# Second layer of a three-layer kernel: output with the tokens on the partitions, states spread in groups of four tiles, and the additions of the lag products on GpSimd

## What is computed

```
ctx      = causal_ema(x, tau_ctx)
gated    = x * sigmoid([x, ctx] @ Wg.T + bg)
h1       = gelu(x @ Wn1.T + bn1)
mod      = 0.5 + sigmoid(h1 @ Wn2.T + bn2)                 # one value per token and trace
traces_d = causal_ema(gated * mod_d, tau_d)                # 32 traces, a = exp(-softplus(tau_d))
temporal = sum_d blend_w[d] * traces_d
gate     = sigmoid(temporal @ Wtemp.T + btemp)
soma     = gelu(x @ Wsoma.T + bsoma)
out      = (soma * gate) @ Wout.T
x        = x + (out - mean(out)) / sqrt(var(out) + 1e-5) * gamma + beta
```

## Time and profile before

| | |
|---|---|
| runs | 2219.94, 2221.18, 2221.75 us; median 2221.18 |
| the profiled execution | span 2220.5 us from the first to the last instruction; its time outside the profiler is not given apart from the three above |
| layer 1, layer 2, layer 3 | about 0 to 938, 938 to 1704, 1704 to 2220 us |
| busy over the span | PE 2051.3 (92%), DVE 1699.0 (77%), ACT 1196.2 (54%), POOL 796.4 (36%) |
| mean granted clock of PE | 0.974 of full speed |

### The profile page before, as it was taken

How to read it: one execution, slowest core, us unless ns; L and a number is a source line. 1 busy time by engine, 2 the same in 40 slices (tenths; PEclk the granted TensorE clock), 3 DMA queues, 4 the chain that set the end, 5 groups by cost and what they waited for, 6 DMA issues and landing times. The chain is left out here.

```text
span 2220.5 us, 42789 instructions
## 1 busy us (share of the span) xinstructions
PE 2051.3 (92%) x14158; PEld 1652.1 (74%) x14158; DVE 1699.0 (77%) x2530; ACT 1196.2 (54%) x2428; POOL 796.4 (36%) x589
## 2 busy tenths in 40 slices
PE   3899999999999999759999999999995999999998
PEld 2566666666666666447777777777774999999997
DVE  6788888888888888577878888887875566666664
ACT  2466565666665666435555555555554555555553
POOL 4645444444455554033333333333340111111111
PEclk8999999999999999879999999999997999999998
DMA  3444444444444444100000000000001222222221
GB/s 92 106 106 107 107 110 110 108 109 108 105 105 106 108 109 104 24 25 1 0 0 0 0 0 0 0 0 0 0 0 59 78 79 70 85 69 80 85 66 60
DMA packets 121171, 137.47 MB, mean 62 GB/s; under 512 B 24240, under 2 KB 89776, under 8 KB 121136
## 3 DMA queue, kind: packets, MB, share of 16 engines
q1 hardware_dynamic: 118576, 128.64, 22.9%
q0 software_dynamic: 2560, 8.39, 1.0%
HBM read 48.35 MB, written 8.39 MB: 26 GB/s over the span
## 5 line engine op out<-in xcount | busy, mean ns | idle before, releaser
L366 DVE TENSOR_REDUCE a_neg_max<-a_s 128x2 f32<-128x512 f32 x512 | 329.1, 683 | 123.4 <-PE a_s L613 121.8
L487 ACT ACTIVATE a_e<-a_t 128x512 f32<-128x512 f32 x512 | 281.2, 610 | 228.4 <-PE a_t L626 228.4
L375 DVE SCALAR_TENSOR_TENSOR a_e<-a_e,a_w_t 128x1024 f32<-128x1024 f32 x256 | 373.6, 1469 | 4.1 <-ACT a_e L487 4.1
L613 PE MATMUL a_s<-a_k_st,a_q_st 96*128 96x256 f32 x1024 | 275.4, 380 | 0.0
L613 PEld LDWEIGHTS a_s<-a_k_st,a_q_st 96*128 96x128 f32 x1024 | 203.5, 199 | 13.7
L610 PE MATMUL a_s<-a_add_m,ident_bf 128*128 128x512 bf16 x512 | 201.8, 394 | 7.9 <-POOL a_add_m L254 5.8
L1695 ACT ACTIVATE c_hid<-c_pH,c_b 128x256 f32<-128x256 f32 x256 | 107.4, 471 | 186.3 <-PE c_pH L1758 185.9
L897 POOL TENSOR_TENSOR b_decayed<-b_table,b_mod_t 128x1024 f32<-128x1024 f32 x64 | 118.6, 1872 | 210.3 <-ACT b_mod_t L1163 203.0
L1317 PE MATMUL b_pS<-b_gated_t,b_decayed 128*128 128x256 f32 x768 | 189.5, 390 | 0.7
L626 PE MATMUL a_t<-a_q_st,a_k_st 97*128 97x512 f32 x512 | 177.1, 426 | 2.6 <-DMA a_q_st<-a_max_row 2.0
L642 PE MATMUL a_v<-a_e,a_v_pad 128*32 128x256 f32 x2048 | 163.6, 392 | 4.5 <-DVE a_e L375 2.1
(11 more groups left out here) (261 smaller groups left out, 5720.4 us busy)
## 6 DMA issues: line engine op xcount, KB each, us to landing
a_q_st<-a_q_hi SPq DMA_DIRECT2D x256, 128.0 KB, 2.4
a_k_st<-a_k_hi SPq DMA_DIRECT2D x256, 64.0 KB, 2.0
a_q_st<-a_q_lo SPq DMA_DIRECT2D x128, 128.0 KB, 2.4
a_xs<-in_xT SPq DMA_DIRECT2D x32, 256.0 KB, 2.8
a_k_st<-a_k_lo SPq DMA_DIRECT2D x128, 64.0 KB, 2.1
x_all<-in_xT SPq DMA_DIRECT2D x32, 256.0 KB, 2.8
c_we<-in_we SPq DMA_DIRECT2D x32, 256.0 KB, 2.7
c_key_t<-in_keyT SPq DMA_DIRECT2D x32, 256.0 KB, 3.2
```

The source lines that it names most:

```text
L366: dve.tensor_reduce(neg_max[:, qc, head:head + 2], ps_s[b][:], AX.X, ALU.max, negate=True).then_inc(red_done, 1)
L375: dve.scalar_tensor_tensor(out=buf[:], in0=buf[:], scalar=BIG, in1=w_t[par][:, kc].unsqueeze(1).to_broadcast([P, 4, S]), op0=ALU.min, op1= ...
L487: act.activation(e[g % E_BUFS][:, 2 * b:2 * b + 2], ps_t[b][:], ACT.Exp).then_inc(exp_done, 1)
L613: ins = pe.matmul(ps_s[b][:, r], q_st[par][0:96, slot, qc * P:qc * P + P], k_st[par][0:96, slot // 2], start=False, stop=(r == 1))
```

## The change

In the trace layer alone:
- `output` swaps its operands: the mixed activations are stationary and `Wout` moves, so `b_pZ` has the tokens on the partitions. The sum of squares over the channels is then along the free axis: ACT's Square with `accum_out` gives `var`, 128x2, and the matmuls of `mean_square` go. The root and the reciprocal are of 128x2. `normalized` (two ACT copies with a scale per partition, into `normed`, which lies in the tile of `wtemp`) takes the place of DVE's product, and `turn_normed` (four PE transposes, into `b_pB`) brings the channels back to the partitions. `scaling` reads `b_pB` and writes `scaled`, which lies in the tile of `wsoma`.
- `spread` is called twice with four tiles instead of four times with two, with four `state` buffers.
- The additions of the lag products are POOL's (`lag_add`), between its low parts and `residual`, with `decays` in the middle.
- The orders of PE, DVE, ACT and POOL are written anew.

```diff
@@ POOL
+        def lag_add(n, lag):
+            pool.wait_ge(prod_done, STEP * n + lag + 1)
+            if lag > 1:
+                pool.wait_ge(inner_done, (STEP - 1) * n + lag - 1)
+            pr = rows(prod[lag % 2]).rearrange("p (a j) -> p a j", j=STEP)[:, :, 0:STEP - lag]
+            y = rows(inner).rearrange("p (a j) -> p a j", j=STEP)[:, :, lag:STEP]
+            pool.tensor_tensor(y, y, pr, ALU.add).then_inc(inner_done, 1)
         def body(n, par, has_a, has_c):
             if has_a:
-                low_inputs(n + 1, 1 - par)
+                low_x(n + 1, 1 - par)
+                low_context(n + 1)
+            for lag in range(1, 5):
+                lag_add(n, lag)
+            if has_a:
                 decays(n + 1, 1 - par)
+            for lag in range(5, STEP):
+                lag_add(n, lag)
             if has_c:
                 residual(n - 1)
@@ DVE
+            if lag > 2:
+                dve.wait_ge(inner_done, (STEP - 1) * n + lag - 2)
             dve.tensor_tensor(pr, g[:, :, 0:STEP - lag], m[:, :, 0:STEP - lag], ALU.mult).then_inc(prod_done, 1)
-            dve.wait_ge(prod_done, STEP * n + lag + 1)
-            ...
-            dve.tensor_tensor(y, y, pr, ALU.add).then_inc(inner_done, 1)
-        def norm(n):
+        def inverse(n):
             dve.wait_ge(std_done, n + 1)
             at_least(dve, normed_done, n)
             dve.reciprocal(rstd[:], std[:]).then_inc(rstd_done, 1)
-            ...
-            dve.tensor_tensor(normed[:], pZ[:], rstd[:].unsqueeze(1).to_broadcast([P, C, S]), ALU.mult).then_inc(normed_done, 1)
         def body(n, par, has_a, has_c):
             states(n, 1)
             lag_sum(n, par, 0)
+            lag_sum(n, par, 1)
             if has_c:
                 mixing(n - 1)
-            lag_sum(n, par, 1)
+            lag_sum(n, par, 2)
+            lag_sum(n, par, 3)
+            states(n, 2)
             if has_c:
                 low_mixed(n - 1)
-            lag_sum(n, par, 2)
-            lag_sum(n, par, 3)
+            states(n, 3)
             if has_a:
                 modulation(n + 1, 1 - par)
-            states(n, 2)
             lag_sum(n, par, 4)
+            lag_sum(n, par, 5)
             if has_c:
-                norm(n - 1)
-            states(n, 3)
-            lag_sum(n, par, 5)
+                inverse(n - 1)
@@ ACT
+        def deviation(n):
             act.wait_ge(out_mm, n + 1)
+            for m in range(C):
+                act.activation(square[:], pZ[:, m], ACT.Square, accum_out=var[:, m:m + 1]).then_inc(sq_done, 1)
+                act.wait_ge(sq_done, C * n + m + 1)
             at_least(act, rstd_done, n)
-            act.activation(std[:], pB[:, 0], ACT.Sqrt, bias=eps[:]).then_inc(std_done, 1)
+            act.activation(std[:], var[:], ACT.Sqrt, bias=eps[:], scale=1.0 / D).then_inc(std_done, 1)
 
             act.activation(table_pick[:], eps[:], ACT.Gelu)
+        def normalized(n):
+            act.wait_ge(rstd_done, n + 1)
+            at_least(act, back_done, n)
+            for m in range(C):
+                ins = act.activation(normed[:, m], pZ[:, m], ACT.Copy, scale=rstd[:, m:m + 1])
+            ins.then_inc(normed_done, 1)
@@ PE
+            for j in range(4):
+                ins = pe.matmul(pY[32 * j:32 * j + 32, h], spread_w[:], state[2 * h + j // 2][:, j % 2],
                                 start=True, stop=True, tile_position=(0, 32 * j))
+        def turn_normed(n):
+            pe.wait_ge(tht_done, NB if isinstance(n, int) and n + 3 > NB else n + 3)
+            pe.wait_ge(normed_done, n + 1)
+            for m in range(C):
+                for c in range(C):
+                    ins = pe.transpose(pB[:, c, m * P:m * P + P], normed[:, m, c * P:c * P + P], ident[:])
+            ins.then_inc(back_done, 1)
         def body(n, par, has_a, has_c):
             states(n, par, 1)
+            if has_a:
+                hidden(n + 1, 1 - par)
+                gate_in(n + 1, 1 - par, 0)
             if has_c:
                 gate_out(n - 1)
-            if has_a:
-                hidden(n + 1, 1 - par)
             lags(n, par, 2)
-            if has_a:
-                gate_in(n + 1, 1 - par, 0)
             spread(n, 0)
             lags(n, par, 3)
             if has_a:
                 modulate_rows(n + 1)
+            states(n, par, 2)
+            states(n, par, 3)
             if has_c:
                 output(n - 1)
             if has_a:
                 modulate_cols(n + 1)
-            spread(n, 1)
-            states(n, par, 2)
-            if has_c:
-                mean_square(n - 1)
             lags(n, par, 4)
             if has_a:
                 gate_in(n + 1, 1 - par, 1)
             lags(n, par, 5)
-            states(n, par, 3)
-            spread(n, 2)
+            spread(n, 1)
             lags(n, par, 6)
-            spread(n, 3)
+            if has_c:
+                turn_normed(n - 1)
             lags(n, par, 7)
```

More of the change, by code:

```diff
@@ L811, in trace_layer @@
     decayed = [sb(f"decayed{i}", [P, TABLE, TRACES]) for i in range(2)]
-    state = [sb(f"state{i}", [P, 2, D]) for i in range(2)]
+    state = [sb(f"state{i}", [P, 2, D]) for i in range(4)]
     inner = sb("inner", [P, C, S])
@@ L819, in trace_layer @@
     mixed = sb("mixed", [P, C, S])
-    square = sb("square", [P, C, S])
-    std = sb("std", [P, S])
-    rstd = sb("rstd", [P, S])
-    normed = sb("normed", [P, C, S])
-    scaled = sb("scaled", [P, C, S])
+    square = sb("square", [P, D])
+    var = sb("var", [P, C])
+    std = sb("std", [P, C])
+    rstd = sb("rstd", [P, C])
+    normed = wtemp
+    scaled = wsoma
     pA = ps("pA", [P, C, S])
@@ L942, in _ @@
         link(dve.memset(eps[:], 1e-5))
[L943 removed]
+        link(dve.memset(var[:], 0.0))
         for tau in (tau_c, tau_col, tau_row):
@@ L1093, in _ @@
         low_mixed(NB - 1)
-        norm(NB - 1)
+        inverse(NB - 1)
     @block.scalar
@@ L1226, in body @@
             if has_c:
-                squares(n - 1)
                 deviation(n - 1)
@@ L1231, in body @@
             if has_c:
+                normalized(n - 1)
                 scaling(n - 1)
@@ L1248, in _ @@
         high_mixed(NB - 1)
-        squares(NB - 1)
         deviation(NB - 1)
+        normalized(NB - 1)
         scaling(NB - 1)
@@ L1319, in states, with spread @@
             ins.then_inc(st_done, 1)
-        def spread(n, q):
-            pe.wait_ge(sw_done, 4 * n + q + 1)
-            if q == 0:
+        def spread(n, h):
+            pe.wait_ge(sw_done, 4 * n + 2 * h + 2)
+            if h == 0:
                 at_least(pe, tho_done, n)
-            for i in range(2):
-                j = (2 * q + i) % 4
-                ins = pe.matmul(pY[32 * j:32 * j + 32, q // 2], spread_w[:], state[q % 2][:, i],
+            for j in range(4):
+                ins = pe.matmul(pY[32 * j:32 * j + 32, h], spread_w[:], state[2 * h + j // 2][:, j % 2],
                                 start=True, stop=True, tile_position=(0, 32 * j))
@@ L1363, in output @@
             for m in range(C):
-                ins = product(pZ[:, m], wout_p, mixed_p, [(k, k) for k in range(C)], m)
+                ins = product(pZ[:, m], mixed_p, wout_p, [(k, k) for k in range(C)], m)
             ins.then_inc(out_mm, 1)
-        def mean_square(n):
+        def turn_normed(n):
             pe.wait_ge(tht_done, NB if isinstance(n, int) and n + 3 > NB else n + 3)
-            pe.wait_ge(sq_done, n + 1)
-            for k in range(C):
-                ins = pe.matmul(pB[:, 0], mean_mat[:], square[:, k], start=(k == 0), stop=(k == C - 1))
-            ins.then_inc(var_mm, 1)
+            pe.wait_ge(normed_done, n + 1)
[3 more added lines that the diff above has]
+            ins.then_inc(back_done, 1)
         def body(n, par, has_a, has_c):
@@ L1425, in _ @@
         output(NB - 1)
-        mean_square(NB - 1)
+        turn_normed(NB - 1)
 HIDDEN = 1024
```

36 lines of the change are left out of this document (13 added, 23 removed).

## The result

The changed kernel takes 2358.76 us (median of 4 runs, 2357.31 to 2361.89), the kernel before 2221.47 (4 runs): slower by a ratio of 1.0624, 95% interval 1.0609 to 1.0639. The forecast was 2327, with a range of 2295 to 2352. The direction and the three waits were right; the time lies 32 us above the forecast and 7 above the range.

What follows compares the result with a forecast made beforehand. PE was taken as the bound in layer 2, busy 94% at full clock, its in-order waits deciding. Profiled span 2220.5 plus 78 for the new order and its waits plus 28 for the clock gave 2327 us, range 2295 to 2352.

Steps and rivals of the forecast that it cites:

- the three waits: PE in each layer 2 batch: 1.4 us for `b_ctx_lo`, about 0.9 before spread 0, 3.2 for `normed` before `turn_normed`.
- the clock term: Layer 2's loop: half clock after the `normed` wait in 7 of 10 batches, 1.35 us each, +28; bounds nothing to +45.
- the clock holds: Rival: the same PE waits in layer 2 but no slow stretch, 2299 us; chance 0.25.
- The waits, +78 forecast: Layer 2: PE's new order with its waits makes a batch 24.95 instead of 22.28 us; +80, less 2 for the end.
- ACT's chain: From `output` to `normed`: squares, two table loads of 1.28, root, `table_pick`, `input_gate`, scaled copies; `turn_normed` can start at 22.0 us.
- The rival by which ACT stands behind each load: ACT stands still after each table load as long as it took: 2.56 us a batch more, 2406; chance 0.02.
- POOL and the port: Rival: POOL's additions or the port shared with DVE delay `low_mixed` and `output`; 2348 at twice the price; chance 0.10.
- DVE's relief is worth at most that wait: DVE loses 3.8 us of additions a batch, worth at most PE's old 1.33 us wait for `b_temp_lo` before `gate_out`.
- "Faster", 2203: Rival: `normed` is there when PE reaches `turn_normed`, a batch takes 21.75 us, 0.53 less than before; chance 0.05.

Runs made afterwards that it cites:

- e3_fill24: The changed kernel with 24 unused matmuls put in front of `turn_normed`'s wait on PE: 2291.4 us, ratio 1.0318 to the kernel before.
- e7_old_order: The changed kernel's arithmetic with the PE and DVE orders of the kernel before, and the additions on DVE: 2181.3 us, ratio 0.9823 to the kernel before.
- e4_adds_dve: The changed kernel with the seven additions of the lag products moved back from POOL to DVE: 2361.3 us, ratio 1.0629 to the kernel before.
- e11: The changed kernel, additions on POOL included, with the PE and DVE orders of the kernel before: 2198.2 us, ratio 0.9892 to the kernel before.
- e9: The changed kernel with newly written orders on four engines and the seven additions back on DVE: 2187.3 us, ratio 0.9848 to the kernel before.
- e8: The changed kernel with newly written orders on PE, DVE, ACT and POOL, additions on POOL: 2128.6 us, ratio 0.9588 to the kernel before.
- e5_before_adds_pool: The kernel before with only the seven additions of the lag products moved to POOL: 2234.6 us, ratio 1.0067 to the kernel before.
- e1: The changed kernel with `output` and `modulate_cols` ahead of states 3 on PE, `low_mixed` and `modulation` ahead of states 2 on DVE: 2257.2 us.
- e2: The changed kernel with ACT's `normalized` moved ahead of `input_gate`, nothing else: 2293.9 us, ratio 1.0331 to the kernel before.
- e10_fill12: The changed kernel with 12 unused matmuls put in front of `turn_normed`'s wait on PE: 2294.5 us, ratio 1.0324 to the kernel before.

## Why the prediction was wrong

The sum was 2220.5 + 78 + 28 = 2327; measured are 2221.2 + 70 + 67 = 2358.8.

**The step that failed is the clock term: +28, with a bound of +45; it measured +67.** I took the 3.4 us at 0.50 from the last batch as the length of a fall, with "a fall in 7 of 10 batches and 1.35 each", and at most 1.5 in every batch. In the loop both were larger: 30 falls with the first 31 waits, 22 of them of some 6.8 us. Of such a fall 5.8 us lie on work; from `turn_normed` to the next lag 0 it takes 5.43 instead of the 2.96 of full clock, and the whole batch 27.30 instead of the 24.69 of e3_fill24, so a long fall costs 2.6 us. Over 31 batches 67.3 us are 2.2 each. The one example I had came from a place where only one wait was seen, and I took it for the size of the mechanism. The term should have been bounded by the work behind the wait: 2.96 us at full clock, times 0.215 / 0.12 by the prediction's own spacings, is 2.3 more a batch, so +73 was the honest upper end, not +45. That a wait for `normed` brings the clock down, and where, was right. Why the same wait of 3.16 is followed by 6.8, by 3.4 or by no slow stretch stays open.

**The rival "the clock holds", 2299**, is the forecast without that term, and e3_fill24 measured it: 2291.4.

**The waits, +78 forecast, +70 measured.** Their lengths and places came as worked out. What was too dear is the work between: states 2 and 3 were priced at 1.83 each, and took 3.27 together (1377.30 to 1380.57), 0.4 less a batch or 12 us in all. In the earlier trace rows the 1.83 of one of them holds what follows too: in the old order with the new operations, states 3 take 1.54 when lag 6 follows. The spreads were mispriced as well. I had 0.5 for a pair and 0.64 to 0.68 for four tiles, a saving of 0.7 a batch; four tiles take 0.57 here (1384.62 to 1385.19), and a pair took 0.55 before:

```profile
1319.21 0.63 PE L1328 MATMUL b_pY<-b_state,b_spread_w 128*32 128x256 f32 x4
1319.76 1.99 PE L1317 MATMUL b_pS<-b_gated_t,b_decayed 128*128 128x256 f32 x8
```

So two spreads of four save 1.1, not 0.7. In e7_old_order states and spreads each take 0.4 to 0.5 us a batch less than I had priced, which is why it came out 13 us below its expectation.

**ACT's chain.** The squares start 16.2 after lag 0 (forecast 16.35), the table loads take 1.28 each, `normalized` begins 20.9 after it (21.05). The rival by which ACT stands behind each load falls: the next activation starts 0.02 and 0.01 us after the load's end. The Trainium skill's drain of 1.38 ("ScalarE: Activation LUTs", section "What ACT_TABLE_LOAD costs") isn't there in the trace of this kernel either; the measurement decides.

**POOL and the port.** In the changed kernel nothing waits for the additions, and e4_adds_dve shows that their place is worth nothing there, as forecast. It is worth something once the wait for `normed` is gone: the additions on POOL cost 17 us in the old order (e11 over e7, `output` starts 0.5 later; whether by the port isn't shown) and save 59 in the new one (e9 over e8, where an addition on DVE meets the decays, and the additions of lags 1 and 2 on DVE put off `low_mixed`).

**"DVE's relief is worth at most that wait"** held: e5_before_adds_pool gained nothing. **"Faster", 2203, if `normed` were there in time** was tested by no run alone: e7_old_order (2181.3) and e8_new_order (2128.6) have no wait for `normed` that comes back every batch, but other orders too. That a shorter wait gains time is shown by e1 and e2.

## What to carry to other kernels

Before taking a slow result for the price of new operations, put them in the old order: here the same arithmetic was 6.2% slower or 1.1% faster than before by the order of two engines alone. When a wait is forecast in a loop on PE, price the clock by the work that stands right behind the wait, at its price at half clock (here 1.8 times), and test it by filling the wait with matmuls that nobody uses. Put the start of a long chain over other engines (here `output`) as early in PE's order as its inputs allow, and heavy POOL operations where DVE doesn't read two SBUF tiles.

## What the runs showed of the hardware that I had not expected

- The fall of the clock isn't in proportion to the idle time. With a longest wait of 1.4 to 1.6 us a batch, layer 2 ran at 1.00; with 2.4 at 0.97; with 3.2 at 0.90. With one piece of 1.6 left of the 3.2 (e10_fill12), the kernel was 3 us slower than with hardly any, and not 34.
- A slow stretch outlasts the wait that brought it by more than 5 us: PE was back at work at 1361.56 and got its clock back at about 1367.4. Where such falls came in every batch, a batch took 27.2 us on average. And the same wait of 3.16 was once followed by no fall at all.
- Work that nobody needs made a kernel faster by 2.9% (e3_fill24 against the changed kernel).
- A DVE addition of 256 elements took 2.31 us on average instead of 0.47 while POOL was multiplying 1024 elements; a scaling of states with one operand in PSUM ran beside POOL's work in its usual 0.68.
- A spread of four tiles, on all four groups of 32 columns, took PE 0.57 us, and one of two tiles 0.55.
